# The first mixture stage of a two-layer kernel: shared layer split around the experts, router turned, one barrier in place of three

## What is computed

```python
shared = silu(xf @ w1) * (xf @ w3) @ w2                       # 4096 tokens, 256 -> 512 -> 256
s = sigmoid(concat([xf, tf], -1) @ router_W)                  # tf: the condition of the token's position, 8 experts
_, topk_idx = top_k(s + router_bias, 2)
s_sel = take_along_axis(s, topk_idx, axis=1)
gates = where(denom > 1e-9, s_sel / (denom + 1e-9), 0.5)      # denom = s_sel.sum(1)
h = gelu(einsum('nc,ech->enh', xf, W1e)); y = einsum('enh,ehc->enc', h, W2e)
routed = einsum('ne,enc->nc', combine, y)                     # gates at the chosen experts
out = (shared + routed) / 3                                   # then batch statistics over all tokens
```

## Time and profile before

| | us |
|---|---|
| median of three timings | 3138.75 (3138.17 to 3141.75) |
| profiled execution, its own time | 3137.02 |
| its span | 3135.1 |
| PE busy | 2886.9 (92%) |
| DVE busy | 1923.6 (61%) |
| ACT busy | 1186.5 (38%) |
| POOL busy | 491.4 (16%) |

### The profile page before, as it was taken

One profiled execution on the slowest core, in us unless ns is written; L12 is line 12 of the kernel. 1 busy time (PEld: TensorE's weight loads), 2 busy tenths in 40 slices (PEclk: granted clock), 3 DMA queues, 4 the chain that ended last, 5 costly groups with the idle time before them and its releaser, 6 DMA issues.

```text
span 3135.1 us, 72707 instructions
## 1 busy us (share of the span) xinstructions
PE 2886.9 (92%) x28718; PEld 2247.6 (72%) x28718; DVE 1923.6 (61%) x6645; ACT 1186.5 (38%) x2696; POOL 491.4 (16%) x645
## 2 busy tenths in 40 slices
PE   7999969999999999999999999758999848999997
PEld 5588658777777777777777776335666638999996
DVE  3245358777777777777777777345677644444443
ACT  0133222333333333333333333224555514555553
POOL 0366000000000000000000000012333223333332
PEclk9999969999999999999999999869999969999998
DMA  3122340101111011010110111111221122222223
GB/s 133 54 87 87 121 180 5 35 19 35 31 23 35 19 35 32 22 35 23 32 32 22 35 28 26 38 28 39 69 73 60 47 101 45 38 38 38 38 37 80
DMA packets 89666, 153.05 MB, mean 49 GB/s; under 512 B 17152, under 2 KB 72320, under 8 KB 86176
## 3 DMA queue, kind: packets, MB, share of 16 engines
q1 hardware_dynamic: 68736, 111.04, 12.5%
q0 software_dynamic: 20448, 37.32, 5.6%
q10 hardware_dynamic: 144, 0.03, 0.0%
HBM read 100.07 MB, written 52.46 MB: 49 GB/s over the span
## 4 chain that ended last, share of the span: by engine, by line
PE 73%; DVE 6%; DMA 2%; ACT 2%; issue 2%; SPq 1%; POOL 1%; POOLq 0%; DVEq 0%; ACTq 0%
PE ps L851 15%; PE ps L675 14%; PE ps L912 8%; PE ps L1812 8%; PE ps L1827 8%; PE ps L834 3%; PE ps L885 3%; PE ps L703 2%; PE ps L704 2%; PE ps L1325 1%; PE ps L1221 1%; PE ps L1281 1%; PE ps L1346 1%; PE ps L1397 1%; PE ps L1258 1%
## 5 line engine op out<-in xcount | busy, mean ns | idle before, releaser
L675 PEld LDWEIGHTS ps<-arena 128*128 128x128 f32 x4096 | 535.3, 192 | 29.0 <-issue 2.5
L851 PE MATMUL ps<-arena 128*128 128x256 f32 x2048 | 551.6, 393 | 0.5 <-DVE arena L861 0.4
L675 PE MATMUL ps<-arena 128*128 128x128 f32 x4096 | 537.9, 275 | 1.9 <-ACT arena L683 1.9
L851 PEld LDWEIGHTS ps<-arena 128*128 128x128 f32 x2048 | 355.9, 191 | 160.8 <-issue 129.8
L683 ACT ACTIVATE arena<-ps 128x256 f32<-128x256 f32 x512 | 192.1, 381 | 466.8 <-PE ps L675 465.7
L912 PE MATMUL ps<-arena 128*16 128x256 f32 x4096 | 283.3, 396 | 31.6 <-DVE arena L942 31.2
L1812 PE MATMUL ps<-arena 128*128 128x128 f32 x2272 | 267.0, 276 | 0.7 <-DVE arena L1884 0.7
L1553 POOL MEMSET arena<- 128x3072 f32 x1 | 2.7, 2657 | 1678.8 <-PE ps L851 1678.8
L1812 PEld LDWEIGHTS ps<-arena 128*128 128x128 f32 x2272 | 260.9, 193 | 1.2 <-DVE arena L1884 1.1
L1827 PE MATMUL ps<-arena 128*128 128x256 f32 x1136 | 256.8, 380 | 0.0
L933 DVE SCALAR_TENSOR_TENSOR arena<-arena 128x128 f32<-128x128 f32 x256 | 73.8, 288 | 288.9 <-ACT arena L924 288.8
(11 more groups left out here) (272 smaller groups left out, 4798.4 us busy)
## 6 DMA issues: line engine op xcount, KB each, us to landing
xw_scratch<-arena SPq DMA_DIRECT2D x32, 512.0 KB, 2.6
arena<-xw_scratch SPq DMA_DIRECT2D x128, 128.0 KB, 4.2
arena<-in_W SPq DMA_DIRECT2D x16, 1024.0 KB, 5.2
arena<-ys_scratch SPq DMA_DIRECT2D x16, 512.0 KB, 8.7
x_scratch<-arena SPq DMA_DIRECT2D x64, 128.0 KB, 2.2
xn_scratch<-arena SPq DMA_DIRECT2D x32, 129.0 KB, 2.7
arena<-in_xT SPq DMA_DIRECT2D x8, 512.0 KB, 8.1
arena<-in_kinT SPq DMA_DIRECT2D x1, 4096.0 KB, 14.5
```

What stands on the lines that cost most here:

```text
L675: m = e.matmul(bank(b)[:, 128 * i:128 * i + 128], kin[:, k, 2 * jp + i, :], xcT[:, k, 128 * blk:128 * blk + 128], start=(k == 0), stop=(k ...
L851: m = e.matmul(bank(7)[:, 0:256], G[blk % 2][:, j, :], kout[:, j, :], start=(j == 0), stop=(j == 31))
```

## The change

- **Blocks.** Three shared blocks (0 to 2) come before the experts and five (3 to 7) after. They begin before the router: xT0 and w1, w3, w2 are loaded first.
- **Router.** rW, padded to 32 columns, is the stationary operand; 512 tokens move; four blocks write four groups of 32 PSUM partitions. 16 products. ACT copies, PE transposes back (8), DVE adds the condition's part for half of the tokens at a time.
- **Top two.** Maximum, equality, and the descending index `r8` to break ties, twice, each over all 256 values (`highest_vector`); the steps stand between the hidden products of block 1.
- **Assignment.** Cut in three functions, placed between hidden products; the four inversions stand one behind each up product of block 2. The second mixture's call is the same work.
- **Down product.** w2 is stationary, 512 tokens move: 8 products, result already transposed, which ACT writes times a third into `xcT`. `sh` is gone.
- **Combine.** ACT scales the first y row, DVE adds the second, PE transposes, DVE adds a third of it to `xcT`, in blocks 4 to 7, two groups of rows in each. y buffers (`ya`) are reused: groups 4 to 7 are loaded when transposes of 0 to 3 are done.
- **ayb** has eight buffers instead of four.
- **Key products** stand between the up products of block 3; kin, Wx, lb, h0, Wh are loaded behind the first y rows, kout behind the keys in two pieces, and awaited at the first L851.
- **Barriers.** One instead of three ahead of the peer stage. Behind it: statistics of the last group, aggregate, scale, memsets.

PE, beginning of the program, before: the last of the router products, the assignment (L138, L139), the first shared products (L247, L248).

```diff
+        spare_at = arena.at
+        silu_s, hs = take(512), take(4, 512)
+        wq, kT = take(16, 256), take(16, 64)
+        assert arena.at <= spare_at + 8192
+        arena.at = spare_at + 8192
...
+        NYA = 8
...
+        def up_tensor_a(e, n, c):
             x_ = xT[:, :, 512 * n:512 * n + 512]
...
+            u, i = 2 * (c % 2), 4 * n + c
+            if c == 0:
+                e.wait_ge(s[f"in{n}"], 16)
+            for w, b, freed in ((w1, u, "sh_si"), (w3, u + 1, "sh_hs")):
+                if i == 0:
+                    e.wait_ge(s["shw"], 48)
+                if i >= 2:
+                    e.wait_ge(s[freed], i - 1)
+                if n == 3 and c < 2:
+                    e.wait_ge(s["a_hb" if c == 0 else "a_hid"], NBK)
+                e.matmul(bank(b), w[:, 0, 128 * c:128 * c + 128], x_[:, 0, :], start=True, stop=False)
+                e.matmul(bank(b), w[:, 1, 128 * c:128 * c + 128], x_[:, 1, :], start=False, stop=True
+                         ).then_inc(s["sh_u"], 1)
+        def down_tensor_a(e, n, h):
+            if h == 0:
+                e.wait_ge(s["sh_hs"], 4 * n + 4)
+            if n:
+                e.wait_ge(s["sh_cp"], 2 * n - 1 + h)
+            if n == 3:
+                e.wait_ge(s["a_y"], NBK)
             for c in range(4):
...
+                m = e.matmul(bank(4 + h), w2[:, c, 128 * h:128 * h + 128], hs[:, c, :], start=(c == 0), stop=(c == 3))
+            m.then_inc(s["sh_dn"], 1)
...
+        def down_scalar_a(e, n, h):
+            e.wait_ge(s["sh_dn"], 2 * n + h + 1)
+            e.activation(xcT[:, h, 512 * n:512 * n + 512], bank(4 + h), ACT.Copy, scale=THIRD).then_inc(s["sh_cp"], 1)
...
+        def router_tensor(e):
+            e.wait_ge(s["rw"], 48)
+            e.matmul(bank(5)[:, 0:8], cT[:, 0, :], rW[:, 2, 0:8], start=True, stop=False)
+            e.matmul(bank(5)[:, 0:8], cT[:, 1, :], rW[:, 3, 0:8], start=False, stop=True).then_inc(s["r_lg"], 1)
+            for i in range(2):
+                for k in range(2):
+                    for g in range(4):
+                        n = 4 * i + g
+                        if k == 0:
+                            e.wait_ge(s[f"in{n}"], 16)
+                        m = e.matmul(bank(6 + i)[32 * g:32 * g + 32, :], rW[:, k, :], xT[:, k, 512 * n:512 * n + 512],
+                                     start=(k == 0), stop=(k == 1))
+                m.then_inc(s["r_lg"], 1)
+        def router_scalar(e, i):
+            e.wait_ge(s["r_lg"], i + 2)
+            e.activation(lgT[:, i], bank(6 + i), ACT.Copy).then_inc(s["r_ev"], 1)
+        def router_back_tensor(e):
+            e.wait_ge(s["tri"], 80)
+            for i in range(2):
+                e.wait_ge(s["r_ev"], i + 1)
+                for j in range(4):
+                    m = e.transpose(bank(6 + i)[:, 128 * j:128 * j + 128], lgT[:, i, 128 * j:128 * j + 128], ident)
+                m.then_inc(s["r_tr"], 1)
+        def cond_vector(e):
+            e.wait_ge(s["r_lg"], 1)
+            e.tensor_copy(TL, bank(5)[:, 0:8]).then_inc(s["rd"], 1)
...
+        def logits_vector(e):
+            rd = s["rd"]
+            e.wait_ge(rd, 1)
+            for i in range(2):
+                e.wait_ge(s["r_tr"], i + 1)
+                e.tensor_tensor(sl4[:, i].rearrange("p j g e -> p g j e"),
+                                bank(6 + i).rearrange("p (j g e) -> p g j e", j=4, g=4)[:, :, :, 0:8],
+                                TL.unsqueeze(1).unsqueeze(1).to_broadcast([128, 4, 4, 8]), ALU.add).then_inc(rd, 1)
...
+        def highest_vector(e, k, o):
+            rd = s["rd"]
+            e.wait_ge(rd, k)
+            e.tensor_reduce(m1, sl, AX.X, ALU.max).then_inc(rd, 1)
+            e.wait_ge(rd, k + 1)
+            e.tensor_tensor(key, sl, m1.unsqueeze(2).to_broadcast([128, 32, 8]), ALU.is_equal).then_inc(rd, 1)
+            e.wait_ge(rd, k + 2)
+            e.tensor_tensor(key, key, r8.unsqueeze(1).to_broadcast([128, 32, 8]), ALU.mult).then_inc(rd, 1)
+            e.wait_ge(rd, k + 3)
+            e.tensor_reduce(m1, key, AX.X, ALU.max).then_inc(rd, 1)
+            e.wait_ge(rd, k + 4)
+            e.tensor_tensor(o, r8.unsqueeze(1).to_broadcast([128, 32, 8]), m1.unsqueeze(2).to_broadcast([128, 32, 8]),
+                            ALU.is_equal).then_inc(rd, 1)
...
-            if n >= 4:
-                e.wait_ge(s[f"ys{n % 4}"], 16 * (n // 4))
-            e.tensor_copy(ayb[n % 4], bank(4 + n % 2)[:, 0:256]).then_inc(s["a_y"], 1)
+            if n >= NYA:
+                e.wait_ge(s[f"ys{n % NYA}"], 16 * (n // NYA))
+            e.tensor_copy(ayb[n % NYA], bank(4 + n % 2)[:, 0:256]).then_inc(s["a_y"], 1)
...
+        def weigh_scalar(e, n):
+            e.wait_ge(s["rg"], 12)
+            e.wait_ge(s[f"in{n}"], 48)
+            for m in range(4 * n, 4 * n + 4):
+                x = e.activation(ya[m][:, 0], ya[m][:, 0], ACT.Copy, scale=g12[:, 0, m:m + 1])
+            x.then_inc(s["ym"], 1)
+        def weigh_vector(e, n):
+            e.wait_ge(s["ym"], n + 1)
+            e.wait_ge(s[f"in{n}"], 48)
+            for m in range(4 * n, 4 * n + 4):
+                x = e.scalar_tensor_tensor(ya[m][:, 0], ya[m][:, 1], g12[:, 1, m:m + 1], ya[m][:, 0], ALU.mult, ALU.add)
+            x.then_inc(s["cb"], 1)
+        def rows_tensor_a(e, n):
+            e.wait_ge(s["cb"], n + 1)
+            if n == 0:
+                e.wait_ge(s["kc"], 4)
+            for c in range(2):
+                if n:
+                    e.wait_ge(s["cx"], 2 * n - 1 + c)
+                for j in range(4):
+                    m = e.transpose(bank(6 + c)[:, 128 * j:128 * j + 128], ya[4 * n + j][:, 0, 128 * c:128 * c + 128], ident)
+                m.then_inc(s["c_tr"], 1)
+        def rows_vector_a(e, n):
+            for c in range(2):
+                x_ = xcT[:, c, 512 * n:512 * n + 512]
+                e.wait_ge(s["c_tr"], 2 * n + c + 1)
+                e.wait_ge(s["sh_cp"], 2 * n + c + 1)
+                e.scalar_tensor_tensor(x_, bank(6 + c), THIRD, x_, ALU.mult, ALU.add).then_inc(s["cx"], 1)
...
+            for c in range(4):
+                up_tensor_a(e, 0, c)
+            router_tensor(e)
+            down_tensor_a(e, 0, 0)
+            router_back_tensor(e)
+            e.wait_ge(s["rd"], 1)
+            down_tensor_a(e, 0, 1)
+            for c in range(4):
+                up_tensor_a(e, 1, c)
+                if c == 2:
+                    e.wait_ge(s["tri"], 80)
+                    e.wait_ge(s["ones"], 2)
+                    assign_tensor(e, s["rd"], 15, oo)
+            down_tensor_a(e, 1, 0)
+            down_tensor_a(e, 1, 1)
+            for c in range(4):
+                up_tensor_a(e, 2, c)
+                invert_tensor(e, 0, c, 7, a_oh, a_bk)
+            down_tensor_a(e, 2, 0)
+            down_tensor_a(e, 2, 1)
+            e.wait_ge(s["sh_hs"], 12)
             expert_head_tensor(e, 0)
             for n in range(NBK + 1):
                 if n + 1 < NBK:
@@ -417,95 +559,74 @@
                 if n < NBK:
                     expert_up_tensor(e, n)
                 if n == 1:
-                    e.wait_ge(s["sh_cp"], 10)
+                    e.wait_ge(s["sh_cp"], 6)
...
+            for n in range(3, 8):
+                for c in range(4):
+                    up_tensor_a(e, n, c)
+                    if n == 3:
+                        keys_tensor(e, c)
+                    elif c % 2:
+                        rows_tensor_a(e, 2 * (n - 4) + c // 2)
+                down_tensor_a(e, n, 0)
+                down_tensor_a(e, n, 1)
...
+            for c in range(4):
+                hidden_vector_a(e, 0, c)
+            cond_vector(e)
+            logits_vector(e)
+            first_vector(e)
+            hidden_vector_a(e, 1, 0)
+            second_vector(e)
+            hidden_vector_a(e, 1, 1)
+            chosen_vector(e)
+            hidden_vector_a(e, 1, 2)
+            assign_counts_vector(e, rd, 15, 1, oo, cum, tot, pre_, cnt8, cntu, nb8, end8)
+            hidden_vector_a(e, 1, 3)
+            assign_slots_vector(e, rd, 15, o1, o2, cum, tot, pre_, nb8, sf)
+            invert_start_vector(e, rd, 15, 0, a_bu, a_bf)
+            for c in range(4):
+                invert_vector(e, 0, c, a_bf, a_oh, a_bk)
+                hidden_vector_a(e, 2, c)
+            assign_experts_vector(e, rd, 15, end8, cmp_, eidf)
+            gates_vector(e)
...
+            for c in range(4):
+                hidden_vector_a(e, 3, c)
+                if c < 3:
+                    keys_vector(e, c)
+            for n in range(4, 8):
+                a = 2 * (n - 4)
+                hidden_vector_a(e, n, 0)
+                if n == 4:
+                    keys_vector(e, 3)
+                weigh_vector(e, a)
+                hidden_vector_a(e, n, 1)
+                weigh_vector(e, a + 1)
+                hidden_vector_a(e, n, 2)
+                rows_vector_a(e, a)
+                hidden_vector_a(e, n, 3)
+                stats_vector(e, a)
+                rows_vector_a(e, a + 1)
```

(31 more changed lines are left out.)

462 lines of the change are left out of this document (181 added, 281 removed).

## The result

| | before | after | ratio, 95% interval |
|---|---|---|---|
| first chip, median us | 3138.46 (4 runs, 3137.4 to 3141.75) | 3091.1 (4 runs, 3086.9 to 3098.9) | 0.985 [0.9829, 0.9871] |
| the same two kernels, chip 14 | 3180.03 (9 runs) | 3126.43 (5 runs) | 0.9829 [0.9816, 0.9843] |
| the same, chip 1 | 3180.35 (9 runs) | 3127.49 (5 runs) | 0.9839 [0.9823, 0.9854] |

The forecast was 3094, range 3087 to 3106; the median is 3091.1, 47.4 us faster than before. The profiled execution took 3091.15, span 3089.3.

The account below looks back on a forecast made before the run. The start of PE's peer stage (445.00 us) was taken to set the end, the 2690 us behind it unchanged. Starting 45.5 sooner (22.8 ahead of the barrier, 22.9 behind) gave 3091.5, on the median 3093.3; with small waits 3094, range 3087 to 3106.

Parts of the forecast that it names:

- The bound that was taken: Router: four column groups overlap as in the recurrent product, so 16 products take 4.0 us, not 13.8.
- Rival A: Router: column groups run one behind another, first gather and end 9.8 us later, 3104; chance 0.08.
- Table switches: ACT in the front: Silu, Sigmoid, Silu, each load 1.28 us; with the skill page's drain up to 2.8 us more.
- The start of the program: PE waits for 2 MB until about 9.5 us, then starts cold at half rate for 4.4 us, costing 2.2.
- The pause: Experts: PE stands still about 20 us, 105 to 127, eight y buffers full until the first store at 124.5.
- costs nothing: Experts: low clock after the pause puts PE 3 to 5 us behind, regained at 0.6 a tile before tile 46.
- Tail: End of experts: from tile 47 (228.1) PE paces at 1.98 us a tile; first shared product behind at 273.3.
- rival B: Shared blocks: combine doesn't fit between products, PE waits 8 to 12 us in all, 3104; chance 0.12.
- rival D: Barrier's far side: a transfer still ends last, up to 5 us more, 3099; chance 0.07.
- the chain of the scale: Behind the barrier: batch norm statistics, aggregate, root, memsets, small steps and xn take 6.1 us against 29.0 before.
- Rival C: Experts: clock falls in the pause and stays at half, 3.96 us a tile, 99 us later, 3193; chance 0.03.
- the allowance for small waits: Whole front: sixty rounded-away waits of 0.05 us, worth 1 or 2 us, added to reach 3094.

Follow-up runs that it names:

- e2_again: Changed kernel with GpSimd gathering 12 tiles instead of 32 before its first store, on chip 12: 3080.66 us, 13.1 faster than the changed kernel by gains.
- e7: Changed kernel with five shared blocks ahead of the experts and three behind, keys in block 3 ahead, on chip 12: 3076.46 us, 17.3 faster by gains.
- e5: Changed kernel with six loads (kin, Wx, bias, h0, Wh, kout) issued behind the first barrier, key products still ahead, chip 12: 3103.78 us, 10.0 slower by gains.
- e1: Changed kernel with its router in the old form (products of 8 moving columns) in the new place, on chip 14: 3149.11 us, 22.7 slower.
- e10: Changed kernel with four blocks ahead and four behind, 27 gathers ahead, first combine group two up products later, chip 1: 3114.14 us, 13.4 faster.

## Why the prediction was right, step by step

| step | forecast | trace |
|---|---|---|
| first product of PE | 9.5 | 9.80 |
| up products of block 0 end | 25.5 | 25.65 |
| 16 router products | 4.0 | 3.57 (26.09 to 29.66) |
| up products of block 1 begin | 37.8 | 37.51 |
| last inversion ends | 78.3 | 78.05 |
| first gather | 84.2 | 83.55 |
| first store | 124.5 | 124.59 |
| y copy that ends the pause | 127.0 | 127.78 |
| first shared product behind the experts | 273.3 | 272.01 |
| block 3 ends | 300.9 | 299.76 |
| a block with two combine groups | 22.65 | 22.52 |
| barrier | 393.3 | 391.5 |
| barrier to first peer product | 6.1 | 6.2 |
| first peer product | 399.5 | 397.70 |
| the rest | 2690.1 | 2691.6 |

- **Router.** The bound that was taken, from the earlier trace rows, was the right one: four column groups run beside each other, 16 products in 3.57 us where one behind another would be 13.8. Rival A fell. The Trainium skill, TensorEngine Tiling (Array Packing), "Theoretical Speedup", gives a factor of up to 4 for a dimension of 32; the trace has 3.9.
- **Table switches.** Load 1.28 and the sigmoid 0.02 behind it (34.01, 35.31), as in the earlier trace rows. The Trainium skill, ScalarE: Activation LUTs, "What ACT_TABLE_LOAD costs", would have had a drain of 1.38 there; the measurement decides, there is none. The prediction has the sum by the page's figure up to 2.8 higher. Less than that would have reached the end: behind its first six passes DVE stood idle for 2.66 us, until PE's next product (41.20).
- **The start of the program** was sized from both sides and landed: half rate from 9.80 to about 14.5, 4.7 us (4.4 forecast).
- **The pause** ended as forecast (first store 124.59, y copy 127.78), but it is 17.3 us long where about 20 were announced, and it began at 111.9 where 105 was. Of these 7 us, 2.7 are the eighth y copy (107.73); the rest is that PE went on behind it by the products of two tiles more, whose results stay in PSUM, before it needed DVE. This cost the forecast nothing, since the end of the pause is set by POOL. The sentence that the pause "costs nothing" is the one that failed in part. As a sentence on the clock it stands by the pace: PE, at clock 0.50 from 129.23 to 133.20, was back at 1.98 a tile from there, had caught up with the pairs of POOL at 141.69, where it waits again, and the pairs, 2.58 apart, set the tiles until 225. As a sentence on the pause itself it doesn't: e2_again removes it and gains 13 us, since what stands behind it is 20 stores that POOL puts off. The forecast held because the walk had the pause in it; a cheaper order was at hand in the same numbers.
- **Tail.** 1.3 us better at its start. The pairs are not the reason: the copy of tile 46, at their end, came at 225.59 (225.5 forecast). Behind it tile 48 followed tile 47 by 1.26 us and the last tile followed by 0.86, where the sum had 1.98 for each. Another 0.5 lie in the pitch of blocks 4 to 7 (22.52 for 22.65). Two groups to a block fit, DVE's and ACT's parts in time: rival B fell for this kernel, and e7 shows a tail where it holds.
- **Behind the barrier.** No transfer ended last (rival D fell), and 6.2 us is the chain of the scale (the terms of the prediction add up to 5.9, not to its 6.1; likewise its last inversion to 78.5, not 78.3). e5 is its test.
- **Rival C.** It fell: low for about 4 us behind the pause, then full, and the table of after has 0.99 for 129 to 272.
- **The stages behind** took 1.5 us more than in the trace of before.

47.3 us sooner at the first peer product (45.5 forecast), less those 1.5, is 45.8, and the two profiled executions differ by 3137.02 - 3091.15 = 45.9. That the gain is met to 0.4 us is in part luck: the front came 1.8 us better than forecast and the stages behind 1.5 worse. Of the 2.9 between 3094 and the median of 3091.1, 1.7 are the step from the profiled execution of before to its median, which the kernel after doesn't have (3091.15, 3091.1), and 0.7 the allowance for small waits, which was not needed; 0.4 are the gain. The four timings lie 12 us apart, so a miss or a hit of 3 us in the median says little; the table above is the better witness.

## What to carry to other kernels

Walk each engine through the new order with durations from rows of the same form, and price the new pause as a place for work, not as free: here it took one number, how many gathers POOL issues ahead of its first store, to turn 13 us of it into time. When a product has few moving columns, count its starts in the timeline against those of a wide one, because the clock can halve under it with the engine busy all along. Look at what a transfer behind a barrier holds up once the compute beside it is gone: of the 22.9 us gained there, 14.4 hung on the early loads, with the key products already ahead (e5); the loads alone, with the key products left behind, were not run.

## What the runs showed of the hardware that was not expected

- The granted clock fell under 8-column products with PE busy without a gap: 0.22 us from start to start until 28.2 us, then 0.43 (e1), and stayed there for the 23 us that the small products lasted.
- In two of the four sessions, on chips 14 and 1, both kernels ran 35 to 42 us slower. During GpSimd's burst of gathers the other engines see TensorE's products up to 26 us late (96.05 to 123.22 in the changed kernel on chip 14), and in e10 on chip 1 TensorE issues singly, at multiples of 0.70 us (103.10 to 121.38). Where a releaser is "remote" or "issue" in such a stretch, the instruction named isn't the cause. Later gathers (2568 to 3070 us in e10, four in a row at most) left TensorE busy for 496.7 of 502 us, against 500.2 in the changed kernel on the first chip. The cause is open; a lack of loaded instructions it is not, by the trace of chip 14.
